# Decoder layer: the last group's feed-forward step computed from all eight experts instead of from fetched expert rows

## The reference, cut to what matters

```python
x = x + ffn(layernorm(x), gate_w, down_w, down_b, up_w, up_b)
# ffn, per sequence b; 8 experts of 64 hidden units, two are chosen:
pooled = x.mean(axis=1)                       # over the 128 rows
gate = softmax(pooled @ gate_w.T)             # 8 numbers
top_w, top_i = top_k(gate, 2)
top_w = top_w / (top_w.sum(axis=-1, keepdims=True) + 1e-08)
h = gelu(einsum('bsd,bkcd->bksc', x, down_w[top_i]) + down_b[top_i])
h = h * top_w
out = einsum('bksc,bkdc->bsd', h, up_w[top_i])
out = out + (top_w * up_b[top_i]).sum(k)
```

## Time and profile before

| | |
|---|---|
| median of three runs | 528.22 us (526.36 to 531.09) |
| span of the profiled execution, its own time | 526.4 us |
| PE, DVE, ACT, POOL busy | 91%, 73%, 68%, 18% of the span |
| end of the last unit's products to the end of the span | 476.8 us to 526.4 us |
| last write to the result in SBUF (line 1031) | ends at 523.84 us |

### The profile page before, as it was taken

One profiled execution on the slowest core, in us unless ns is written; L12 is line 12 of the kernel. 1 busy time (PEld: TensorE's weight loads), 2 busy tenths in 40 slices (PEclk: granted clock), 3 DMA queues, 4 the chain that ended last, 5 costly groups with the idle time before them and its releaser, 6 DMA issues. The chain is left out here.

```text
span 526.4 us, 26012 instructions
## 1 busy us (share of the span) xinstructions
PE 481.6 (91%) x11236; PEld 397.2 (75%) x11236; DVE 382.8 (73%) x1090; ACT 356.7 (68%) x829; POOL 96.8 (18%) x102
## 2 busy tenths in 40 slices
PE   1899999999998899999998899999998999988645
PEld 1687878877887688878887788888887887867534
DVE  5778886766678697784878697785778597773772
ACT  4867777767776857788666877768666867756221
POOL 1112211111112021231111121142012121130120
PEclk9989999999999999999998999999999999989958
DMA  8900000001010010022110010022100010020112
GB/s 321 303 4 4 2 4 4 4 4 42 4 44 2 2 44 4 4 65 62 43 29 18 4 42 4 4 63 63 42 5 3 3 44 4 4 82 3 40 40 80
DMA packets 15264, 20.35 MB, mean 39 GB/s; under 512 B 1200, under 2 KB 12976, under 8 KB 15152
## 3 DMA queue, kind: packets, MB, share of 16 engines
q1 hardware_dynamic: 13872, 14.49, 8.4%
q0 software_dynamic: 1280, 4.20, 2.9%
HBM read 16.60 MB, written 2.10 MB: 36 GB/s over the span
## 5 line engine op out<-in xcount | busy, mean ns | idle before, releaser
L456 ACT COPY states<-states 128x512 f32<-128x512 f32 (+1 forms) x160 | 94.6, 591 | 91.6 <-DVE states L682 85.1
L682 DVE TENSOR_TENSOR states<-states,spans 128x512 f32<-128x512 f32 x128 | 88.4, 690 | 15.0 <-ACT states L456 4.1
L369 POOL TENSOR_TENSOR rnorm<-norm_sq,neg_half 128x4 f32<-128x4 f32 x32 | 33.0, 1032 | 291.1 <-DVE norm_sq L725 291.1
L1194 PE MATMUL acc<-wo_sb,oT_sb 128*128 128x256 f32 x256 | 60.9, 381 | 0.7 <-ACT oT_sb L483 0.7
L1096 PE MATMUL ring<-xnT,wk_sb 128*128 128x512 f32 x192 | 53.7, 415 | 2.0 <-DVE xnT L788 1.6
L1109 PE MATMUL ring<-wv_sb,xnT 128*128 128x256 f32 x384 | 55.0, 292 | 0.2 <-DVE wv_sb L925 0.2
L1096 PE MATMUL ring<-xnT,wq_sb 128*128 128x512 f32 x192 | 53.3, 413 | 0.0
L1096 PE MATMUL ring<-xnT,wg_sb 128*128 128x512 f32 x192 | 52.2, 409 | 0.3 <-DVE wg_sb L925 0.3
L713 DVE COPY_PREDICATED blocks<-owned,lo_bank 128x128 f32<-128x128 uint32 x128 | 38.5, 301 | 18.9 <-PE lo_bank L1119 14.9
L1194 PEld LDWEIGHTS acc<-wo_sb,oT_sb 128*128 128x128 f32 x256 | 46.4, 192 | 5.9 <-ACT oT_sb L483 0.9
L1109 PEld LDWEIGHTS ring<-wv_sb,xnT 128*128 128x128 f32 x384 | 48.4, 190 | 0.8 <-DVE wv_sb L925 0.3
(11 more groups left out here) (160 smaller groups left out, 875.9 us busy)
## 6 DMA issues: line engine op xcount, KB each, us to landing
x_buf<-x_dram SPq DMA_DIRECT2D x4, 512.0 KB, 4.1
ctxT_sb<-ctxT_dram SPq DMA_DIRECT2D x8, 256.0 KB, 4.0
ctx_sb<-ctx_dram SPq DMA_DIRECT2D x4, 512.0 KB, 4.6
out_dram<-x_mid SPq DMA_DIRECT2D x6, 256.0 KB, 2.3
states<-wk_dram SPq DMA_DIRECT2D x1, 1024.0 KB, 5.9
states<-wg_dram SPq DMA_DIRECT2D x1, 1024.0 KB, 8.0
states<-wq_dram SPq DMA_DIRECT2D x1, 1024.0 KB, 10.0
v_sb<-wv_dram SPq DMA_DIRECT2D x1, 1024.0 KB, 12.1
```

What stands on the lines that cost most here:

```text
L369: nc.gpsimd.tensor_tensor(rnorm[:, m % 4, GB:2 * GB], norm_sq[:, GB:2 * GB], neg_half[:, GB:2 * GB], ALU.pow).then_inc(rk_set, 1)
L456: nc.scalar.copy(dst, src).then_inc(carry_set, 1)
L682: nc.vector.tensor_tensor(dst, src, by, ALU.mult).then_inc(decayed, 1)
L1194: last = mm(accs[z][:, D * m:D * m + D], oT_sb[:, n % 2, T * b:T * b + T], wo_sb[:, h], start=(h == 0 and m == 0), stop=(h == H - 1 and m ...
```

## The change

For the last group alone, nothing is fetched by row. When the last level product is done, SP loads the down weights of all eight experts (`down_all`, 512 KB) and their up weights (`up_all`, 512 KB) into `states`, and a table of biases comes with the constants at the start. The 512 hidden units are 4 blocks of 128 (`UNITS` = 4); PE makes them all for both halves, ACT applies gelu to blocks of 128 x 256, and DVE multiplies each sequence's 4 blocks with a weight per unit (`unit_w`), which is zero for experts that are not chosen. The up projection is then 4 products a sequence where it was one. The sums over the rows for the gate come from PE: `half_pool` takes `xn` as weights and a column of ones. DVE's order around it changes: the previous group's last residual (`tail_part(U, "end")`, line 873) goes behind `half_rsum(0)`.

```diff
@@ SP
-            for dst, src in ((owned, owned_c), (lanes, lanes_c)):
+            for dst, src in ((owned, owned_c), (lanes, lanes_c), (dense_bias, bias_all)):
                 sp.dma_start(dst[:], src).then_inc(c_in, 16)
...
+            sp.wait_ge(level_mm, LEVELS * U)
+            sp.dma_start(dense_down, down_all.rearrange("(c p) u -> p c u", p=P)).then_inc(dense_in, 16)
+            sp.dma_start(dense_up, up_all.rearrange("(j p) d -> p j d", p=P)).then_inc(dense_in, 16)
@@ POOL
-            for z in range(2):
-                fetch_experts(NG - 1, (2 * z, 2 * z + 1), z)
@@ ACT
             def half_gelu(z):
                 act.wait_ge(half_mm[z], MM_HID)
-                for m in range(2):
-                    b = 2 * z + m
-                    last = nc.scalar.activation(hidden[:, b], half_bank[z][1][:, T * m:T * m + T], ACT.Gelu,
-                                                bias=sel[:, b, 2 * D:2 * D + 1])
+                for j in range(UNITS):
+                    src = half_bank[z][1] if j < 2 else ring_of(("dense", NG - 1, z))
+                    at = 2 * T * (j % 2)
+                    last = nc.scalar.activation(dense_hidden[:, j, 2 * T * z:2 * T * z + 2 * T], src[:, at:at + 2 * T],
+                                                ACT.Gelu, bias=dense_bias[:, j:j + 1])
                 last.then_inc(half_out[z], 1)
@@
-            half_rows(0, TO_X3T)
-            half_rows(1, TO_X3T)
             for z in range(2):
+                half_rows(z, TO_X3T)
                 gate_exp_out(t, slice(2 * z, 2 * z + 2), z)
             nc.scalar.activation(warm[:], neg_half[:, 0:1], ACT.Gelu)
-            downT_out(t, 0)
+            act.wait_ge(c_in, N_C)
             half_gelu(0)
-            downT_out(t, 1)
             half_gelu(1)
@@ DVE
+            def unit_weights(of):
+                count = of.stop - of.start
+                shape = [P, count, TOP_K, UNITS]
+                link(nc.vector.tensor_copy(top_f[:, of], top_idx[:, of, 0:TOP_K]))
+                link(nc.vector.tensor_tensor(chosen_k[:, of], top_f[:, of].unsqueeze(3).broadcast_to(shape),
+                                             lanes[:, 2:2 + UNITS].unsqueeze(1).unsqueeze(1).broadcast_to(shape),
+                                             ALU.is_equal))
+                link(nc.vector.tensor_tensor(chosen_k[:, of], chosen_k[:, of],
+                                             top_w[:, of].unsqueeze(3).broadcast_to(shape), ALU.mult))
+                nc.vector.tensor_tensor(unit_w[:, of], chosen_k[:, of, 0], chosen_k[:, of, 1],
+                                        ALU.add).then_inc(unit_w_set, 1)
+
+            def weigh_hidden(z):
+                dve.wait_ge(half_out[z], TO_GELU)
+                dve.wait_ge(unit_w_set, z + 1)
+                for b in (2 * z, 2 * z + 1):
+                    units = dense_hidden[:, :, T * b:T * b + T]
+                    nc.vector.tensor_tensor(units, units, unit_w[:, b].unsqueeze(2).broadcast_to([P, UNITS, T]),
+                                            ALU.mult).then_inc(up_set, 1)
@@
-            def half_pooled(z):
-                dve.wait_ge(half_out[z], TO_X3T)
-                src = rowsT[:, :, 2 * T * z:2 * T * z + 2 * T].rearrange("p c (b t) -> p c b t", b=2)
-                done(nc.vector.tensor_reduce(pooled[:, :, 2 * z:2 * z + 2], src, AX, ALU.add), z)
+            def half_gate_products(z):
+                dve.wait_ge(half_mm[z], MM_POOL)
+                sums = half_bank[z][0][:, 0:2 * KC].rearrange("p (c b) -> p c b", c=KC)
+                nc.vector.tensor_tensor(gated[:, :, 2 * z:2 * z + 2], sums.unsqueeze(3).broadcast_to([P, KC, 2, E]),
...
@@ PE
+            def half_pool(z):
+                pe.wait_ge(half_row[z], AT_XN2)
+                for c in range(KC):
+                    for m in range(2):
+                        to = 2 * c + m
+                        last = mm(half_bank[z][0][:, to:to + 1], xn[:, 2 * z + m, P * c:P * c + P], ones[:],
+                                  start=True, stop=True)
+                last.then_inc(half_mm[z], 1)
@@
+            def half_hidden(z, js):
+                if js[0] == 0:
+                    pe.wait_ge(half_out[z], TO_X3T)
+                    pe.wait_ge(dense_in, 16 * 2)
+                    bank = half_bank[z][1]
+                else:
+                    bank = fill(("dense", t, z))
+                for j in js:
+                    to = 2 * T * (j % 2)
+                    for c in range(KC):
+                        last = mm(bank[:, to:to + 2 * T], dense_down[:, c, P * j:P * j + P],
+                                  rowsT[:, c, 2 * T * z:2 * T * z + 2 * T], start=(c == 0), stop=(c == KC - 1))
+                if js[-1] == UNITS - 1:
+                    last.then_inc(half_mm[z], 1)
+
+            def half_up(z):
                 for m in range(2):
                     b = 2 * z + m
+                    pe.wait_ge(up_set, NG - 1 + b + 1)
+                    for j in range(UNITS):
+                        last = mm(half_bank[z][0][:, D * m:D * m + D], dense_hidden[:, j, T * b:T * b + T], dense_up[:, j],
+                                  start=False, stop=(m == 1 and j == UNITS - 1))
                 last.then_inc(half_mm[z], 1)
```

More of the change, by code:

```diff
@@ L221, in fill_order @@
             order.extend(tail_slot(U, "B"))
-            order.extend((kind, NG - 1, z) for kind in ("gate", "downT") for z in range(2))
+            order.extend((kind, NG - 1, z) for z in range(2) for kind in ("gate", "dense"))
             return order
@@ L228, in decoder_kernel @@
         for name in ORDER:
-            if len(name) == 3:
+            if len(name) == 3 and name[0] != "dense":
                 TAIL[name] = len(TAIL) + 1
@@ L822, in link, with choose @@
                 (wait_first if plain else dve.wait_ge)(small, steps[0])
-            def choose(t, of=slice(0, GB), k=0):
+            def choose(t, of=slice(0, GB), k=0, rows=True):
                 count = of.stop - of.start
@@ L836, in choose @@
                 link(ins)
+                if not rows:
+                    return
                 for z in range(2):
@@ L1041, in _ @@
             half_xn(1, 1)
-            tail_part(U, "end")
             half_max(0)
@@ L1045, in _ @@
             half_rsum(0)
+            tail_part(U, "end")
             half_sum(0, AT_SUM2)
@@ L1389, in _ @@
             half_context(1)
-            half_transposed(0, MM_X3T)
-            half_transposed(1, MM_X3T)
-            for z in range(2):
-                gate(t, slice(2 * z, 2 * z + 2), z).then_inc(tail_mm, 1)
+            def half_pool(z):
[6 more added lines that the diff above has]
+                last.then_inc(half_mm[z], 1)
             def half_bias(z):
@@ L1412, in half_hidden @@
                 last.then_inc(half_mm[z], 1)
-            def half_up(z):
-                pe.wait_ge(half_out[z], TO_GELU)
-                pe.wait_ge(up_set, t + 1 + z)
-                for m in range(2):
-                    b = 2 * z + m
-                    last = mm(half_bank[z][0][:, D * m:D * m + D], hidden[:, b], sel[:, b, D:2 * D],
-                              start=False, stop=(m == 1))
-                last.then_inc(half_mm[z], 1)
+            half_pool(0)
+            half_transposed(0, MM_X3T)
@@ L1423, in _ @@
+            gate(t, slice(0, 2), 0).then_inc(tail_mm, 1)
+            half_hidden(0, (0, 1))
+            half_pool(1)
+            half_transposed(1, MM_X3T)
+            half_hidden(0, (2, 3))
+            gate(t, slice(2, 4), 1).then_inc(tail_mm, 1)
+            half_hidden(1, (0, 1))
+            half_hidden(1, (2, 3))
             half_bias(0)
             half_bias(1)
-            down_transposed(t, 0).then_inc(tail_mm, 1)
-            half_hidden(0)
-            down_transposed(t, 1).then_inc(tail_mm, 1)
@@ L1428, in _ @@
             half_up(0)
-            half_hidden(1)
             half_up(1)
@@ L1441 @@
                              np.expand_dims(L0_ffn_down_b, 2)], axis=2)
+    units = np.reshape(L0_ffn_down_w, (E * BN, D))
     arrays = {
```

68 lines of the change are left out of this document (37 added, 31 removed).

## The result

In the comparison of 18 runs each, the changed kernel took 532.22 us (median) and the kernel before 529.04 us: ratio 1.0063, interval 1.0039 to 1.0087, so 3.3 us slower, within the 1% that the prediction called no change. It didn't reproduce: in two later comparisons the same kernel gave 0.9956 (0.9927 to 0.9985) and 1.0055 (1.0015 to 1.0094). The experiments show that two things move: the end stage, whose length follows its order, its work and the granted clock in it, and the body ahead of it, which the change leaves as it was but for a small table loaded at the start. Runs more than 1.5% above the fastest of the same kernel are not in the ratios: here one of 594.57 us (before) and one of 538.58 us (changed), in the second comparison two of the changed kernel's 12 (with them the ratio of the means is 0.9975), in the third one of 2548 us.

What follows compares the result with a forecast made beforehand. Bound by tiny DVE instructions up to 513.7 us, then PE and ACT steps. Second half's choice +3.1 us, the rest -1.6: 528.2 + 1.5 = 529.7 us, range 525.5 to 532.5.

Steps and rivals of the forecast that it cites:

- The number: Whole kernel: median of the runs 529.7 us, 1.5 us slower than 528.2; within 1% given 85%.
- a clock that returns late: Rival, end stage: PE's clock back at 509.3 us, +2.5 us in all; one case with the forecast, 57% together.
- What bounds: End stage: tiny DVE instructions up to 513.7 us, then PE and ACT steps; row fetch nearly hidden, its removal gives little.
- The dense weights: 1 MB loaded into `states` from 476.8 us, wanted at 503.7 us; no such transfer comes near 27 us.
- The new wait: DVE, before the gate's products of half 1: idles some 3.7 us for PE's sums, behind half 0's first hidden units.
- The clock: PE in the end stage: at half clock from about 500.3 us, back at 506.9 us, bounds 503.5 and 509.3 us.
- Prices: End stage: 256-column instruction 0.216 us at full clock, 0.465 at half; `half_pool` 1.1 and 1.9 us; `unit_weights` 0.8 us.
- The gelu table: ACT, after half 1's exp: load 1.28 us plus 0.2 for first use, the skill's 1.38 us drain left out.
- The sum: End stage: second half's choice 3.1 us later, the rest 8.5 us against 10.1, so 1.5 us slower.
- The body: Everything up to 476.8 us: taken as not touched by the change, so only the end stage was read.
- a body that differs by more than 1 us: Sign: such a difference before 476.8 us would show the prediction wrong in its ground.
- Slower by over 1%: Rival: clock falls again before the up projection, +9.5 us, 535.9 us span, 9%; this outcome 11% in all.

Runs made afterwards that it cites:

- f1_rows_ready: Kernel before, with the last group's rows loaded from a fixed expert pair about 20 us ahead, not fetched by the choice: end stage 39.9 us, ratio 0.9983.
- e1_sums_first: Changed kernel with half 1's sums and transpositions ahead of half 0's first hidden units on PE: end stage 39.3 us, ratio 1.0000.
- e2_gates_first: Changed kernel with all sums, transpositions and both gates ahead of hidden units on PE, half 1's gate products behind half 0's choice: stage 38.4 us, ratio 0.9997.
- g3_wide_only: Changed kernel with sums over the rows using 128 equal columns of ones in place of one, no idle products: end stage 39.4 us, ratio 0.9964.
- f3_busy_before: Kernel before with 18 idle products of 256 columns in PE's gaps up to the second bias product: end stage 36.5 us, ratio 0.9989.
- g2_fetch_pe_sums_busy: Kernel before, rows fetched, with gate sums by PE (128 columns wide), half 1's gate products behind half 0's choice, 13 idle products: stage 35.0 us, ratio 0.9909.

## Why the prediction was right, point by point

- **The number.** 532.22 us lies 0.3 us under the upper end of the range, 532.5, which stood for a clock that returns late and scatter. The clock wasn't late; in the profile 2.0 of the 2.8 us came from the body. That the range held is in good part luck. (Its lower end should read 525.0 by its own terms, 528.2 - 1.5 - 1.7.)

- **What bounds.** The fetch is nearly hidden: shown by f1_rows_ready, 0.5 us at most. The dense weights, put at nothing, ended no wait: PE's first hidden units (505.61 us) follow the gate's products without a gap.
- **The new wait.** Forecast "some 3.7 us", measured 3.71 us. That the order costs it is shown by e1_sums_first (1.10 us), but taking it away gained nothing there, since gate(1) was next, and 0.7 us in e2_gates_first, since PE was next. I had called the wait the cost of the order; what it costs at this clock is 0.7 us, what lies behind it is PE's work.
- **The clock.** Forecast back at 506.9 us, 21.4 us into the stage; measured 21.2 us. The three profiles of the change all have 6.8 us at half clock. The fall was read off rightly from PE's idle time before it (2.12 us, as in the earlier trace rows); the return was a good guess rather than understanding: g3_wide_only, from the same thinking, missed.
- **Prices.** `half_pool` 1.86 and 0.95 us (1.9 and 1.1 forecast); up projection 7.17 us (6.9 + 0.15); `unit_weights` 0.70 us (0.8, bounds 0.65 and 1.0); four gelu blocks 1.55 us (1.6). For these products, which each load 128 columns of weights, the row holds (0.12 us each). The 25 ns that the Trainium skill gives under "TensorE: Matmul & The Clock Gate", section "Back-to-back issue gap", is there the floor of a product's own issue, without the weights.
- **The gelu table.** 1.28 us, and the first use 0.02 us behind it; the drain of "ScalarE: Activation LUTs" in the Trainium skill, section "What ACT_TABLE_LOAD costs", isn't seen in this chain either, and gelu was 0.6 us early.
- **The sum.** Forecast +1.5 us for the stage, measured +0.8: the choice of half 0 could start 22.5 us into the stage and not 22.9, and both halves' weights took 0.2 us less each (0.1 of it in `unit_weights`); behind them 8.65 us and not 8.5. The size of this difference means little, as the stage of before took 40.3 us in another profile: the sum assumed that the half clock of before, 17 us, is a constant.
- **The body.** "The body, up to 476.8 us, is not touched, so I read only the end stage" is the step that failed. Its code is the same, its time isn't: 2.0 us in the first profile, about 4.9 us between two comparisons of one kernel, more than all that the change does to its stage. The prediction had itself named a body that differs by more than 1 us as the sign that it is wrong in its ground, and that sign came.
- **Slower by over 1%** didn't come: the clock stayed at 1.00 under the up projection in all three profiles, with the bias products (1.03 and 1.13 us in the first) in the gap before it.

## What to carry to other kernels

When a wait for data is taken away by computing more, look first whether that wait ends anything, and then add up the engine that does the extra work: here 64 instructions of 256 columns, 13.8 us at full clock, took the place of a fetch that cost at most 0.5 us and of the few products on its rows. An instruction that another engine waits for doesn't belong behind bulk work, though moving it pays only until the next one is late. Where a change is worth under 1%, judge it by the length of its own stage and the granted clock in it, and don't trust an interval from one comparison: three of one kernel gave 1.0063, 0.9956 and 1.0055.

## What the runs showed that I had not expected

- Within the runs of one kernel, time goes with the time at half clock: for the change 522.1 us + 0.48 us for each microsecond at 1.2 GHz (30 runs, scatter 1.0 us), for the kernel before 517.7 + 0.41 (92 runs, 0.7 us). The lines must not be drawn on to full clock, where they would put the change some 4 us behind: no run of the kernel before was below 16.8 us, and the two end stages with the clock at 1.00 are equally long. A microsecond at half clock has no fixed price. In the end stage, where tiny DVE instructions make up much of the chain, 17 us cost 1.8 (f3_busy_before), 0.1 us for each; in the body a fall of 3.4 us at 181 us costs 1.4.
- Products whose results nobody uses made the kernel faster: 1.8 us of the end stage in f3_busy_before. In its median that isn't seen; g2_fetch_pe_sums_busy, which has them too, is faster in its median as well.
- In g3_wide_only PE was busy for 3.39 us from 502.1 to 505.5 us and the clock was still at 0.50 at 508.9 us; in the kernel before it was back after 2.93 busy us of 3.40. What decides stays open.
